# Token mixer written out by batch, with scales kept per batch, entry and shortcut on ScalarE, output products a batch late, and some lag taps as diagonal products on TensorE

## The chip, the cores and the metric

The kernel runs on one core of a Trainium2 chip. The metric is device microseconds of the whole program, lower is better. The median of three runs is 1840.42 us (1838.47 to 1841.76). One more execution was profiled; it took 1830.69 us, and its span from the first to the last instruction is 1828.9 us.

## The reference, cut to what matters

The program is a chain of eight stages on x, of 8 batches, 512 positions and 128 features, in float32. The change touches one stage, the token mixer, which stands between two runs of the same feed-forward. With h as the normalised x:

```python
h  = (x - mean) / sqrt(var + 1e-5)                 # shortcut
xn = h / (rms(h) + 1e-8)
u  = silu(xn @ Wu.T + bu)                          # 256 wide
v  = silu(xn @ Wv.T + bv)                          # 256 wide
o[n]  = sum(coef[lag] * v[n - lag] for lag in 0..n)  # n is the batch; causal
x  = x + (u * o) @ Wo.T + bo + h
```

The mixing runs over the first axis of x, the 8 batches. So batch n needs the v of all batches up to it, and n + 1 taps. The coefficient depends on the feature alone (per partition, with the features laid on partitions). The reference computes this sum by FFT; the kernels compute it by taps.

## The kernel before, in words

x lies in SBUF for the whole program as 32 tiles of 128 positions by 128 features, four tiles a batch. A stage is a block with one program for each engine. Engines meet by semaphores only, and each engine runs its instructions in the order in which its program is written. At the end of a stage all engines meet at a barrier.

The mixer (`token_mixer`, L2343 to L2466) does for each batch: statistics on VectorE (`Norm.stats`, L192 and L196: four and four instructions); on GpSimd a chain of seven small instructions that makes the two factors out of variance and mean (`Norm.powers`, L216 to L223, then `rms_factor`, L2353 to L2357); the normalised x on VectorE (L245) and its scaled copy on ScalarE (L253); four transposes on TensorE (L275) and a copy out of PSUM on ScalarE (L283); four products of 128x512 on TensorE (L2421), each followed by a silu on ScalarE (L2411), two of them u, two of them v; the taps on VectorE, two feature halves of n + 1 taps each, into `mixed` (L2458 for lag 0, L2456 for all others); the product with u (L2462); the output products with the bias on TensorE (L2425, L2429) into one of two PSUM banks by turns; and the sum into x on VectorE (L2446), after GpSimd has added the shortcut (L2399).

The order is written out by `batches`: the front of batch n + 1, then the back of batch n. On VectorE the front is the normalisation of batch n + 1 and the statistics of batch n + 2, and the back is the taps, the product with u, and the sum into x of batch n - 1. On TensorE the front is the transposes and the four products, and the back is the output products of batch n. The v of all batches is kept in `vT`.

The feed-forward stages (`feed_forward`) aren't changed. They are of use here because they hold instructions of the kinds that the changed mixer has: an entry on ScalarE with Identity, a scale and a bias per partition (L2198), and a VectorE instruction with a PSUM input, a scalar per partition and an SBUF input (L2323).

Of the kernel before, what the change touches and what calls it, by code (L numbers as in the profile page):

```python
# [16 lines left out]
F32 = mybir.dt.float32  # L17
# [8 lines left out]
P = 128  # L26
# [2316 lines left out]
def token_mixer(nc, k, name="mix"):  # L2343

    with Stage(nc, name) as st:
        half = st.sb("half", [P, T], F32)
        minus_one = st.sb("minus_one", [P, T], F32)

        def rms_factor(steps, pool, p):
            ms = norm.ms[:, :]
            steps.did(pool.tensor_tensor(ms, ms, half[:, :], ALU.pow))  # L2353
            steps.settle()
            steps.did(pool.tensor_scalar(ms, ms, 1e-8, None, ALU.add))
            steps.settle()
            steps.did(pool.tensor_tensor(norm.factor[:, p, :], ms, minus_one[:, :], ALU.pow))  # L2357

        norm = Norm(st, k.x, 1e-5, "layer_rms", rms_factor, 3)
        bank = [k.ps[:, i, :] for i in range(8)]  # L2360
        feed = Feed(st, k, norm, bank[0])
        ps_uv, ps_out = bank[1:5], bank[5:7]
# [4 lines left out]
        exps = st.counter("exponents")  # L2367
        uv_ready = st.counter("uv_ready", 4, 2)
        silu_ready = st.counter("silu_ready", 4, 1)
        shortcut = st.counter("shortcut_added", 1, 2)  # L2370
        taps = [st.counter(f"taps{c}", 1) for c in range(FEAT)]
        gated_ready = st.counter("gated_ready", FEAT, 2)
        out_ready = st.counter("out_ready", 1, 2)
        x_added = st.counter("x_added", 1, 2)
        norm.also_read = shortcut
        block = st.block()

        def batches(front, back):
            front(0, 0)
            for n in range(B):  # L2380
                if n + 1 < B:
                    front(n + 1, (n + 1) % 2)
                back(n, n % 2)

        @block.sync
        def _(sp):
            st.credit(sp)

        @block.gpsimd
        def _(pool):  # L2390
            norm.setup(pool)
            pool.memset(half[:, :], 0.5)
            pool.memset(minus_one[:, :], -1.0).then_inc(exps.sem, 1)
            hold(pool, exps.sem, 1)

            def back(n, p):
                hold(pool, norm.normed.sem, norm.normed.at(n))
                x = k.x[:, n * T:(n + 1) * T, :]
                pool.tensor_tensor(x, x, norm.out[:, p, :, :], ALU.add).then_inc(shortcut.sem, 1)  # L2399
            batches(lambda n, p: norm.powers(pool, n, p), back)  # L2400

        @block.scalar
        def _(act):
            def front(n, p):
                feed.scalar(act, n, p, uv_ready, uv_ready.at(n - 2))
                for c in range(2 * FEAT):
                    act.wait_ge(uv_ready.sem, uv_ready.at(n, c + 1))
                    if c == 0:
                        act.wait_ge(gated_ready.sem, gated_ready.at(n - 2))
                    to = uT[:, p, c, :] if c < FEAT else vT[:, c - FEAT, n, :]  # L2410
                    act.activation(to, ps_uv[c], ACT.Silu, bias=k.buv[:, c:c + 1]).then_inc(silu_ready.sem, 1)  # L2411
            batches(front, lambda n, p: None)

        @block.tensor
        def _(pe):
            def front(n, p):
                feed.tensor(pe, n, p)
                pe.wait_ge(feed.xT_ready.sem, feed.xT_ready.at(n))
                for c in range(2 * FEAT):
                    pe.wait_ge(silu_ready.sem, silu_ready.at(n - 1, c + 1))  # L2420
                    pe.matmul(ps_uv[c], k.WuvT[:, c * P:(c + 1) * P], feed.xT[:, p, :], start=True, stop=True).then_inc(uv_ready.sem, 1)  # L2421

            def back(n, p):
                pe.wait_ge(x_added.sem, x_added.at(n - 2))
                pe.matmul(ps_out[p], k.onesb, k.bto_rows.unsqueeze(1).to_broadcast([P, T, P]), start=True, stop=True)  # L2425
                for c in range(FEAT):
                    pe.wait_ge(gated_ready.sem, gated_ready.at(n, c + 1))
                    for j in range(T):
                        ins = pe.matmul(ps_out[p][:, j * P:(j + 1) * P], gated[:, p, c, j * P:(j + 1) * P], k.WtoT[:, c * P:(c + 1) * P],  # L2429
                                        start=False, stop=True, skip_group_check=True)  # L2430
                ins.then_inc(out_ready.sem, 1)
            batches(front, back)

        @block.vector
        def _(dve):
            counts = [0] * FEAT

            def did(c, ins):
                ins.then_inc(taps[c].sem, 1)
                counts[c] += 1  # L2440

            def add(n, p):
                dve.wait_ge(out_ready.sem, out_ready.at(n))
                dve.wait_ge(shortcut.sem, shortcut.at(n))
                x = k.x[:, n * T:(n + 1) * T, :].rearrange("p a b -> p (a b)")
                dve.tensor_tensor(x, ps_out[p], x, ALU.add).then_inc(x_added.sem, 1)  # L2446

            def back(n, p):
                dve.wait_ge(silu_ready.sem, silu_ready.at(n))
                dve.wait_ge(gated_ready.sem, gated_ready.at(n - 1))  # L2450
                for lag in range(n + 1):
                    for c in range(FEAT):
# [442 lines left out]
```

## Time and profile before

| | |
|---|---|
| median of 3 runs | 1840.42 us |
| profiled execution | 1830.69 us |
| its span | 1828.9 us |
| busy in the span: TensorE, VectorE, ScalarE, GpSimd | 72%, 59%, 42%, 46% |
| mean granted TensorE clock | 0.854 of full |
| the mixer, from its first VectorE instruction to its last (1618.92 to 1721.46) | 102.54 us |

The busy shares are means over eight stages. The mixer is 6% of the span, between 1618.92 and 1721.46 us. The timeline gives an engine's instructions in order of time, equal ones in a row merged; what stands in square brackets is the time that the engine sat idle before them, with the instruction that ended it. A float32 product on TensorE stands as two records. A granted clock of 1.00 is 2.4 GHz, and 0.50 is 1.2 GHz.

### The profile page before, as it was taken

To read this page: it belongs to the slowest core of one execution; us is meant where nothing else is said; L and a number is where in the kernel's file an instruction comes from. 1 tells how busy PE (TensorE), PEld (TensorE's weight loads), DVE (VectorE), ACT (ScalarE), POOL (GpSimd) and SP (SyncE) were. 2 spreads that over 40 slices of the span, in tenths; PEclk is the share of its full clock that TensorE was granted. 3 is DMA by queue.
4 is the path that set the end of the run, shared out by engine and by line. 5 is a ranking of instruction groups with operands and counts; after the bars stand their busy time and mean duration, and the time that the engine had idled before them with its cause. 6 is when DMAs were issued, how large, how long until landed. Compare 5 with 4: busy or idle time off the path is not lost. (4 is left out here: it accounts for less than half of the span.)

```text
span 1828.9 us, 36163 instructions
## 1 busy us (share of the span) xinstructions
PE 1316.1 (72%) x11164; PEld 849.2 (46%) x11165; DVE 1071.5 (59%) x3170; ACT 774.4 (42%) x1286; POOL 834.1 (46%) x1221
## 2 busy tenths in 40 slices
PE   5763259963988888832299817888899995957486
PEld 3542159961233333322299812333345554734364
DVE  2654425445877877444255456767576634749765
ACT  1221113211466666711033204776655555735274
POOL 2116745533233333357555536766654413447252
PEclk9985579985799999955599956998999998978698
DMA  3004122245323222041122230000000000000001
GB/s 104 0 16 122 42 63 69 67 118 128 71 80 85 66 65 65 3 126 41 58 68 68 59 95 1 1 2 1 2 2 2 1 2 1 1 1 1 1 1 47
DMA packets 87712, 79.80 MB, mean 44 GB/s; under 512 B 11791, under 2 KB 77583, under 8 KB 87280
## 3 DMA queue, kind: packets, MB, share of 16 engines
q1 hardware_dynamic: 76898, 57.16, 12.1%
q0 software_dynamic: 8704, 17.97, 2.9%
q10 hardware_dynamic: 1980, 3.00, 0.8%
q8 instruction: 73, 1.20, 0.3%
q14 instruction: 57, 0.47, 0.1%
HBM read 46.07 MB, written 32.01 MB: 43 GB/s over the span
## 5 line engine op out<-in xcount | busy, mean ns | idle before, releaser
L1146 ACT ACTIVATE grp_pt<-ps 128x1024 f32<-128x1024 f32 (+2 forms) x320 | 244.7, 799 | 212.2 <-PE ps L1223 133.9
L2035 DVE TENSOR_REDUCE soft_mx<-ps 128x2 f32<-128x1024 f32 (+3 forms) x256 | 201.9, 821 | 57.0 <-PE ps L1873 55.7
L680 POOL DMA_INDIRECT products<-moe_product,moe_rows_in x144 | 152.9, 1062 | 151.9 <-DVE moe_product L852 142.3
L1759 ACT ACTIVATE soft_pt<-ps 128x768 f32<-128x768 f32 (+1 forms) x192 | 166.3, 884 | 83.2 <-PE ps L1904 81.6
L707 ACT ACTIVATE moe_hid<-ps 128x512 f32<-128x512 f32 x144 | 85.8, 597 | 249.9 <-PE ps L744 234.2
L1680 POOL TENSOR_SCALAR_AFFINE_SELECT soft_pt<-soft_pt 128x256 f32<-128x256 f32 (+1 forms) x192 | 92.7, 483 | 208.9 <-ACT soft_pt L1759 208.4
L744 PE MATMUL ps<-moe_rT,moe_W_now 128*128 128x128 f32 x1152 | 157.2, 280 | 2.0 <-issue 2.0
L1243 PE MATMUL ps<-grp_pt,grp_vpad 128*32 128x160 f32 (+4 forms) x2048 | 145.6, 393 | 15.9 <-POOL grp_pt L1088 15.7
L753 PE MATMUL ps<-moe_W,moe_hid 128*128 x1152 | 155.2, 278 | 1.3 <-ACT moe_hid L707 1.1
L658 POOL DMA_INDIRECT sorted_rows<-moe_row,moe_target x128 | 124.8, 975 | 50.2 <-issue 35.7
L744 PEld LDWEIGHTS ps<-moe_rT,moe_W_now 128*128 128x128 f32 x1152 | 143.2, 196 | 5.5 <-issue 5.4
L753 PEld LDWEIGHTS ps<-moe_W,moe_hid 128*128 128x128 f32 x1152 | 140.5, 192 | 3.5 <-issue 2.6
L1088 POOL TENSOR_SCALAR_AFFINE_SELECT grp_pt<-grp_pt 128x256 f32<-128x256 f32 (+1 forms) x192 | 102.9, 544 | 70.7 <-ACT grp_pt L1146 69.8
L848 DVE COPY moe_W_now<-moe_W 128x512 f32 x144 | 62.0, 431 | 68.5 <-issue 68.5
L1223 PE MATMUL ps<-grp_qst,grp_kst 32*128 32x160 f16 (+4 forms) x1024 | 96.3, 279 | 7.4 <-ACT grp_pt L1146 5.2
L275 PE MATMUL ps<-pack,moe_normed 128*128 128x128 f32 x64 | 17.8, 433 | 108.2 <-DVE moe_normed L245 108.2
L852 DVE TENSOR_SCALAR moe_product<-ps,moe_rows_in 128x128 f32<-128x128 f32 x144 | 50.6, 351 | 74.2 <-PE ps L753 72.5
L1921 PE MATMUL ps<-soft_pt,soft_vpad 128*32 128x512 f32 (+3 forms) x1024 | 88.8, 442 | 2.1 <-POOL soft_pt L1680 1.9
L1868 PE MATMUL ps<-soft_kst,soft_qst 64*128 64x512 bf16 (+3 forms) x512 | 72.0, 320 | 21.0 <-ACT soft_pt L1759 12.7
L737 PE MATMUL ps<-pack,moe_rows_in 128*128 128x128 f32 x144 | 40.6, 282 | 61.9 <-DMA moe_rows_in<-sorted_rows 61.4
L1243 PEld LDWEIGHTS ps<-grp_pt,grp_vpad 128*32 128x32 f32 x2048 | 51.7, 112 | 61.9 <-POOL grp_pt L1088 24.5
L1223 PEld LDWEIGHTS ps<-grp_qst,grp_kst 32*128 32x128 f16 x1024 | 34.1, 93 | 90.9 <-ACT grp_pt L1146 46.3
(335 smaller groups left out, 2754.2 us busy)
## 6 DMA issues: line engine op xcount, KB each, us to landing
moe_rows_in<-sorted_rows SPq DMA_DIRECT2D x144, 65.0 KB, 1.8
moe_back<-products SPq DMA_DIRECT2D x16, 512.0 KB, 7.2
soft_kst<-soft_scratch_k SPq DMA_DIRECT2D x32, 192.0 KB
moe_W<-in_W SPq DMA_DIRECT2D x2, 2048.0 KB, 8.5
moe_W<-in_W SPq DMA_DIRECT2D x16, 256.0 KB, 6.9
soft_scratch_q<-soft_parts SPq DMA_DIRECT2D x16, 192.0 KB, 2.7
soft_qst<-soft_scratch_q SPq DMA_DIRECT2D x32, 96.0 KB
soft_scratch_k<-soft_parts SPq DMA_DIRECT2D x14, 192.0 KB, 2.8
```

The source lines that it names most:

```text
L658: pool.indirect_dma_start(k.sorted_rows, bass.IndirectOffsetOnAxis(target[:, p, s, j:j + 1], 0), row[:, p, j, s, :], None).then_inc(scatte ...
L680: pool.indirect_dma_start(k.products, bass.IndirectOffsetOnAxis(rows_in[:, u, DEST_COL:DEST_COL + 1].bitcast(U32), 0), product[:, u, :], N ...
L744: ins = pe.matmul(ps_hid[u % 2][:, c * P:(c + 1) * P], W1_now[:, u % 2, c * P:(c + 1) * P], rT[:, u % 2, :], start=True, stop=True)
L753: ins = pe.matmul(ps_out[u % 2][:, 0:P], hid[:, u % 2, c * P:(c + 1) * P], W2[:, bass.ds(e, 1), c * P:(c + 1) * P].rearrange("f a h -> f ( ...
L1088: pool.affine_select(e, e, [[0, 2 if seg < 2 else 4], [1, P]], ALU.is_ge, 0.0, 0, -1).then_inc(kept.sem, 1)
L1146: act.activation(at.pair(pt[:, s % 2, :], pair, seg)[:, :, 0:w], ring[(chunks_before(m) + c) % 2][:, :, 0:w], ACT.Exp, scale=scale).then_i ...
L1223: ins = pe.matmul(ring[now % 2][:, b, col:col + w], kst[32 * g:32 * g + 32, p, j * P:(j + 1) * P], qst[32 * g:32 * g + 32, p, s, j * P:j * ...
L1243: ins = pe.matmul(sums[half][32 * g:32 * g + 32, q:q + w], vpad[:, p, j, par, g, :], at.head(pt[:, s % 2, :], g, seg, a, w), start=(par == ...
L1680: pool.affine_select(e, e, [[0, 2 if seg < 2 else 4], [1, P]], ALU.is_ge, 0.0, 0, -1).then_inc(kept.sem, 1)
L1759: act.activation(LATENT.pair(pt[:, s % 2, :], pair, seg)[:, :, 0:w], ring[second_turn(n, c) % RING3][:, :, 0:w], ACT.Exp, scale=scale).the ...
L1921: ins = pe.matmul(sums[half][32 * g:32 * g + 32, q:q + w], vpad[:, n % 2, par, j, 4 * half + g, :], LATENT.head(pt[:, s % 2, :], g, seg, a ...
L2035: ins = dve.tensor_reduce(mx[:, tile, half, :, r], ring[first_turn(n, d) % RING3][:, :, at:at + keys], AX.X, ALU.max)
```

## The change

The stage gets its own code in place of the shared `Norm` and `Feed`.

- VectorE no longer normalises. It does the statistics two batches ahead, at the start of an iteration, then the taps that are left to it, the product with u, and the sum into x of the batch before.
- GpSimd makes all scales and shifts in a chain of twelve small instructions a batch, kept per batch, and before the second batch six diagonal matrices (the identity times a coefficient). It no longer adds the shortcut.
- ScalarE makes the input of the transposes straight from x (`entries`, with Identity, scale and bias), and turns x into x + h in place (`shortcuts`). The silus of v come ahead of those of u.
- TensorE does the taps of `PE_LAGS` as products of a diagonal matrix with v (11 lags for each of the two feature halves: 22 products of 128x512), a batch ahead; VectorE's first tap adds their sum out of PSUM. The output products of batch n - 1 stand in iteration n, behind the front of batches n + 2 and n + 1 and the taps of n + 1. There is one PSUM bank for them instead of two.

The core of the new code follows; the new `power` also makes `in_scale`, the product of `rstd` and `factor`.

```diff
+    PE_LAGS = [[], [], [1], [1], [1, 2], [1, 2], [1, 2], [1, 2, 3]]
+    DIAGS = 3
+    OUTPUTS = (2, 3, 0, 1)
+    with_taps = [n for n in range(B) if PE_LAGS[n]]
...
+        def taps_through(n):
+            return sum(m + 1 - len(PE_LAGS[m]) for m in range(n))
+        def v_ready(n, c):
+            return silu_ready.at(n, OUTPUTS.index(FEAT + c) + 1)
+        @block.gpsimd
+        def _(pool):
...
+            def power(n):
+                mean, var = mv[:, n, :, 0], mv[:, n, :, 1]
+                pool.wait_ge(stats_done.sem, stats_done.at(n))
+                need(pool, powered, powered.at(n - 1))
+                pool.tensor_scalar(tmp[:, :], var, 1e-5, None, ALU.add).then_inc(powered.sem, 1)
...
+                pool.tensor_tensor(in_shift[:, n, :], tmp[:, :], in_scale[:, n, :], ALU.mult).then_inc(powered.sem, 1)
+                pool.tensor_tensor(x_shift[:, n, :], tmp[:, :], rstd[:, :], ALU.mult).then_inc(powered.sem, 1)
+                pool.tensor_scalar(x_scale[:, n, :], rstd[:, :], 1.0, None, ALU.add).then_inc(powered.sem, 1)
+            power(0)
+            for c in range(FEAT):
+                for lag in range(1, DIAGS + 1):
+                    at = c * B + lag
+                    ins = pool.tensor_scalar(diag[:, c, lag - 1, :], k.ident, k.coef[:, at:at + 1], None, ALU.mult)
+            ins.then_inc(diags_set.sem, 1)
+            for n in range(1, B):
+                power(n)
...
+            def entries(n):
+                p = n % 2
+                act.wait_ge(powered.sem, powered.at(n, 10))
+                need(act, x_turned, x_turned.at(n - 2))
+                for j in range(T):
+                    ins = act.activation(entry[:, p, j, :], k.x[:, n * T + j, :], ACT.Identity, bias=in_shift[:, n, j:j + 1], scale=in_scale[:, n, j:j + 1])
+                ins.then_inc(normed.sem, 1)
+            def shortcuts(n):
+                act.wait_ge(powered.sem, powered.at(n))
+                act.wait_ge(normed.sem, normed.at(n))
+                for j in range(T):
+                    x = k.x[:, n * T + j, :]
+                    ins = act.activation(x, x, ACT.Identity, bias=x_shift[:, n, j:j + 1], scale=x_scale[:, n, j:j + 1])
+                ins.then_inc(shortcut.sem, 1)
+            def copy_xT(n):
+                act.wait_ge(x_turned.sem, x_turned.at(n))
+                need(act, uv_ready, uv_ready.at(n - 2))
+                act.activation(xT[:, n % 2, :], ps_x, ACT.Copy).then_inc(xT_ready.sem, 1)
+            def silus(n):
+                for i, c in enumerate(OUTPUTS):
+                    act.wait_ge(uv_ready.sem, uv_ready.at(n, i + 1))
+                    if c < FEAT:
+                        need(act, gated_ready, gated_ready.at(n - 2, c + 1))
+                    to = uT[:, n % 2, c, :] if c < FEAT else vT[:, c - FEAT, n, :]
+                    act.activation(to, ps_uv[c], ACT.Silu, bias=k.buv[:, c:c + 1]).then_inc(silu_ready.sem, 1)
+            entries(0)
+            copy_xT(0)
+            entries(1)
             for n in range(B):
                 if n + 1 < B:
+                    copy_xT(n + 1)
+                silus(n)
+                shortcuts(n)
+                if n + 2 < B:
+                    entries(n + 2)
...
+            def turn(n):
+                pe.wait_ge(normed.sem, normed.at(n))
+                need(pe, xT_ready, xT_ready.at(n - 1))
+                for j in range(T):
+                    ins = pe.transpose(ps_x[:, j * P:(j + 1) * P], entry[:, n % 2, j, :], k.ident)
+                ins.then_inc(x_turned.sem, 1)
+            def project(n):
+                pe.wait_ge(xT_ready.sem, xT_ready.at(n))
+                for i, c in enumerate(OUTPUTS):
+                    need(pe, silu_ready, silu_ready.at(n - 1, i + 1))
+                    pe.matmul(ps_uv[c], k.WuvT[:, c * P:(c + 1) * P], xT[:, n % 2, :], start=True, stop=True).then_inc(uv_ready.sem, 1)
+            def tap(n):
+                turn_of = with_taps.index(n)
+                pe.wait_ge(diags_set.sem, 1)
+                for c in range(FEAT):
+                    pe.wait_ge(silu_ready.sem, v_ready(n - 1, c))
+                    if turn_of > 0:
+                        pe.wait_ge(taps[c].sem, taps_through(n - 1) + 1)
+                    for i, lag in enumerate(PE_LAGS[n]):
+                        ins = pe.matmul(ps_tap[c], diag[:, c, lag - 1, :], vT[:, c, n - lag, :], start=(i == 0), stop=(i == len(PE_LAGS[n]) - 1))
+                    ins.then_inc(tapped.sem, 1)
+            def output(n):
+                need(pe, x_added, x_added.at(n - 1))
+                pe.matmul(ps_out, k.onesb, k.bto_rows.unsqueeze(1).to_broadcast([P, T, P]), start=True, stop=True)
                 for c in range(FEAT):
                     pe.wait_ge(gated_ready.sem, gated_ready.at(n, c + 1))
                     for j in range(T):
+                        ins = pe.matmul(ps_out[:, j * P:(j + 1) * P], gated[:, n % 2, c, j * P:(j + 1) * P], k.WtoT[:, c * P:(c + 1) * P],
                                         start=False, stop=True, skip_group_check=True)
                 ins.then_inc(out_ready.sem, 1)
...
+            turn(0)
+            turn(1)
+            project(0)
+            for n in range(B):
+                if n + 2 < B:
+                    turn(n + 2)
+                if n + 1 < B:
+                    project(n + 1)
+                if n + 1 in with_taps:
+                    tap(n + 1)
+                if n > 0:
+                    output(n - 1)
+            output(B - 1)
...
+            def stats(n):
+                need(dve, stats_done, stats_done.at(n - 1))
+                for j in range(T):
+                    ins = dve.bn_stats(bn[:, j, :], k.x[:, n * T + j, :])
+                ins.then_inc(stats_done.sem, 1)
+                dve.wait_ge(stats_done.sem, stats_done.at(n, 1))
+                for j in range(T):
+                    ins = dve.bn_aggr(mv[:, n, j, :], bn[:, j, :])
+                ins.then_inc(stats_done.sem, 1)
+            def mix(n):
+                lags = [lag for lag in range(n, -1, -1) if lag not in PE_LAGS[n]]
+                need(dve, gated_ready, gated_ready.at(n - 1))
+                for i, lag in enumerate(lags):
+                    for c in range(FEAT):
+                        at = c * B + lag
+                        v, scale = vT[:, c, n - lag, :], k.coef[:, at:at + 1]
+                        dve.wait_ge(silu_ready.sem, v_ready(n - lag, c))
+                        if i > 0:
+                            dve.wait_ge(taps[c].sem, counts[c])
+                            dve.scalar_tensor_tensor(mixed[:, c, :], v, scale, mixed[:, c, :], ALU.mult, ALU.add).then_inc(taps[c].sem, 1)
+                            counts[c] += 1
+                        elif n in with_taps:
+                            dve.wait_ge(tapped.sem, tapped.at(with_taps.index(n), c + 1))
+                            dve.scalar_tensor_tensor(mixed[:, c, :], v, scale, ps_tap[c], ALU.mult, ALU.add).then_inc(taps[c].sem, 1)
+                            counts[c] += 1
+                        else:
+                            dve.tensor_scalar(mixed[:, c, :], v, scale, None, ALU.mult).then_inc(taps[c].sem, 1)
+                            counts[c] += 1
+            def gate(n):
+                need(dve, out_ready, out_ready.at(n - 2))
+                for c in range(FEAT):
+                    dve.wait_ge(silu_ready.sem, silu_ready.at(n, OUTPUTS.index(c) + 1))
+                    dve.wait_ge(taps[c].sem, counts[c])
+                    dve.tensor_tensor(gated[:, n % 2, c, :], mixed[:, c, :], uT[:, n % 2, c, :], ALU.mult).then_inc(gated_ready.sem, 1)
+            def add(n):
                 dve.wait_ge(out_ready.sem, out_ready.at(n))
                 dve.wait_ge(shortcut.sem, shortcut.at(n))
...
+                x = x_of(n).rearrange("p a b -> p (a b)")
+                dve.tensor_tensor(x, ps_out, x, ALU.add).then_inc(x_added.sem, 1)
+            stats(0)
+            stats(1)
+            for n in range(B):
+                if n + 2 < B:
+                    stats(n + 2)
+                mix(n)
+                gate(n)
+                if n > 0:
+                    add(n - 1)
+            add(B - 1)
```

## Rows read from the trace of the kernel before

**Rows 1.** Stretch: its us; PE, PEld, DVE, ACT, POOL busy (instructions); granted clock; DMA.

```profile
1618.92:1721.46 102.54, 66.25 (x232) 38.78 (x232) 82.87 (x200) 37.91 (x73) 52.99 (x67) 0.75 0.00 1
```

**Rows 2.** Timeline (start, us) of VectorE: the mixer's start and last batches.

```profile
1618.92 0.87 DVE L192 BATCH_NORM_STATS2 mix_bn<-x 128x6 f32<-128x128 f32 x4 [1.60 <-PEq L112]
1619.83 0.38 DVE L196 BATCH_NORM_AGGREGATE mix_mv<-mix_bn 128x2 f32<-128x6 f32 x4
...
1683.90 7.71 DVE L2456 SCALAR_TENSOR_TENSOR mix_mixed<-mix_vT,pack,mix_mixed 128x512 f32<-128x512 f32 x10
...
1705.55 0.68 DVE L2446 TENSOR_TENSOR x<-ps,x 128x512 f32<-128x512 f32 x1
1706.15 0.87 DVE L2458 TENSOR_SCALAR mix_mixed<-mix_vT,pack 128x512 f32<-128x512 f32 x2
1706.94 9.36 DVE L2456 SCALAR_TENSOR_TENSOR mix_mixed<-mix_vT,pack,mix_mixed 128x512 f32<-128x512 f32 x14
1716.21 1.28 DVE L2462 TENSOR_TENSOR mix_gated<-mix_mixed,mix_uT 128x512 f32<-128x512 f32 x2
1717.42 0.68 DVE L2446 TENSOR_TENSOR x<-ps,x 128x512 f32<-128x512 f32 x1
1720.77 0.69 DVE L2446 TENSOR_TENSOR x<-ps,x 128x512 f32<-128x512 f32 x1 [2.67 <-PE ps L2429]
```

**Rows 3.** Timeline of ScalarE in the mixer and the next entry.

```profile
1628.45 0.60 ACT L283 ACTIVATE mix_xT<-ps 128x512 f32<-128x512 f32 x1 [1.21 <-PE ps L275]
...
1700.03 0.69 ACT L2411 ACTIVATE mix_vT<-ps,pack 128x512 f32<-128x512 f32 x1 [0.17 <-PE ps L2421]
...
1726.50 1.65 ACT L2198 ACTIVATE ffn_entry<-x,ffn_xshift,ffn_xrstd 128x128 f32<-128x128 f32 x4 [24.93 <-POOL ffn_xshift L2175]
```

**Rows 4.** Timeline of GpSimd: small instructions of batches 0, 5 and 7.

```profile
1620.36 0.23 POOL L216 TENSOR_SCALAR mix_power_in<-mix_mv 128x4 f32<-128x4 f32 x1 [1.19 <-issue]
...
1623.75 1.04 POOL L2357 TENSOR_TENSOR mix_factor<-mix_ms,mix_minus_one 128x4 f32<-128x4 f32 x1
...
1666.70 1.66 POOL L2355 TENSOR_SCALAR mix_ms<-mix_ms 128x4 f32<-128x4 f32 x1
...
1683.30 0.37 POOL L216 TENSOR_SCALAR mix_power_in<-mix_mv 128x4 f32<-128x4 f32 x1 [2.14 <-DVE mix_mv L196]
...
1688.12 1.39 POOL L2357 TENSOR_TENSOR mix_factor<-mix_ms,mix_minus_one 128x4 f32<-128x4 f32 x1
```

**Rows 5.** Timeline of TensorE in the mixer.

```profile
1629.10 6.29 PE L2421 MATMUL ps<-mix_xT,pack 128*128 128x512 f32 x8 [0.69 <-ACT mix_xT L283]
...
1648.63 3.70 PE L2421 MATMUL ps<-mix_xT,pack 128*128 128x512 f32 x8 [0.69 <-ACT mix_xT L283]
1652.17 0.38 PE L2425 MATMUL ps<-bias_rows,onesb 128*128 128x512 bf16 x1
...
1654.27 0.66 PE L275 MATMUL ps<-pack,mix_normed 128*128 128x128 f32 x4
...
1672.93 1.12 PE L275 MATMUL ps<-pack,mix_normed 128*128 128x128 f32 x4 [3.15 <-ACT mix_normed L253]
1674.73 5.66 PE L2421 MATMUL ps<-mix_xT,pack 128*128 128x512 f32 x8 [0.69 <-ACT mix_xT L283]
...
1716.95 3.78 PE L2429 MATMUL ps<-pack,mix_gated 128*128 128x128 f32 x16 [8.49 <-DVE mix_gated L2462]
```

**Rows 6.** Stretches after one idle time of TensorE.

```profile
1672.00:1674.00 2.00, 1.07 (x4) 0.72 (x4) 1.97 (x9) 0.88 (x4) 1.07 (x2) 0.50 0.00 0
...
1678.00:1680.00 2.00, 2.00 (x5) 0.82 (x4) 2.00 (x5) 1.11 (x2) 2.00 (x2) 0.82 0.00 0
```

**Rows 7.** Groups of GpSimd by shape: busy us, mean ns.

```profile
L1078 POOL COPY grp_vpad<-grp_qkv 128x128 f32<-128x128 f32 x32 | 9.4, 324 | 1.7 <-PE ps L1243 1.7
```

**Rows 8.** Groups of VectorE by shape.

```profile
L2323 DVE SCALAR_TENSOR_TENSOR ffn_h<-ps,pack,ffn_h 128x512 f32<-128x512 f32 x48 | 35.2, 733 | 25.2 <-PE ps L2269 25.2
```

**Rows 9.** Groups of ScalarE by shape.

```profile
L2216 ACT ACT_TABLE_LOAD x2 | 2.6, 1283 | 0.0
```

More of the change, by code:

```diff
@@ L2343, in token_mixer, with need @@
 def token_mixer(nc, k, name="mix"):
-    with Stage(nc, name) as st:
[L2348 to L2359, printed above, removed]
-        bank = [k.ps[:, i, :] for i in range(8)]
-        feed = Feed(st, k, norm, bank[0])
-        ps_uv, ps_out = bank[1:5], bank[5:7]
+    PE_LAGS = [[], [], [1], [1], [1, 2], [1, 2], [1, 2], [1, 2, 3]]
+    DIAGS = 3
+    OUTPUTS = (2, 3, 0, 1)
+    with_taps = [n for n in range(B) if PE_LAGS[n]]
+    def need(eng, signal, value):
+        if value > 0:
+            eng.wait_ge(signal.sem, value)
+    with Stage(nc, name) as st:
+        bank = [k.ps[:, i, :] for i in range(8)]
+        ps_x, ps_uv, ps_out, ps_tap = bank[0], bank[1:5], bank[5], bank[6:8]
+        bn = st.sb("bn", [P, T, 6], F32)
+        mv = st.sb("mv", [P, B, T, 2], F32)
+        tmp = st.sb("tmp", [P, T], F32)
+        rstd = st.sb("rstd", [P, T], F32)
+        factor = st.sb("factor", [P, T], F32)
+        half = st.sb("half", [P, 3, T], F32)
+        in_scale = st.sb("in_scale", [P, B, T], F32)
+        in_shift = st.sb("in_shift", [P, B, T], F32)
+        x_scale = st.sb("x_scale", [P, B, T], F32)
+        x_shift = st.sb("x_shift", [P, B, T], F32)
+        entry = st.sb("entry", [P, 2, T, P], F32)
+        xT = st.sb("xT", [P, 2, S], F32)
+        diag = st.sb("diag", [P, FEAT, DIAGS, P], F32)
         vT = st.sb("vT", [P, FEAT, B, S], F32)
@@ L2366, in token_mixer @@
         gated = st.sb("gated", [P, 2, FEAT, S], F32)
[L2367 to L2375, printed above, removed]
@@ L2376, in token_mixer @@
-        block = st.block()
-        def batches(front, back):
-            front(0, 0)
+        exps = st.counter("exponents", 3)
+        diags_set = st.counter("diags_set")
+        stats_done = st.counter("stats_done", 2)
+        powered = st.counter("power_steps", 12)
+        normed = st.counter("normed")
+        shortcut = st.counter("shortcut")
+        x_turned = st.counter("x_turned")
+        xT_ready = st.counter("xT_ready")
+        uv_ready = st.counter("uv_ready", 4)
+        silu_ready = st.counter("silu_ready", 4)
@@ L2402, in _ @@
[L2402 to L2412, printed above, removed]
+                    copy_xT(n + 1)
@@ L2466, in _ @@
-            norm.stats(dve, 0, 0)
-            batches(lambda n, p: feed.vector(dve, n, p), back)
-            add(B - 1, (B - 1) % 2)
+                x = x_of(n).rearrange("p a b -> p (a b)")
[9 more added lines that the diff above has]
+                    add(n - 1)
```

79 lines of the change are left out of this document (29 added, 50 removed).

## The prediction

> **What bounds the kernel now.** I read the views in this order. The page first: no engine is busy for more than 72% of the span, and the mixer is a small part of it, so only the mixer's own stretch counts. Then that stretch by itself [rows 1]: 102.54 us, in which VectorE is busy for 82.87, TensorE for 66.25, GpSimd for 52.99 and ScalarE for 37.91, at a mean granted clock of 0.75. VectorE paces it: in the timeline its late batches stand end to end, with the taps of the last batch at 1706.94 right behind the sum at 1705.55 and the product with u right behind them [rows 2]. The reader is to see what VectorE does not wait for: the scales of the next batches are made on GpSimd while VectorE is at the taps of this one. Last, the timelines of GpSimd, ScalarE and TensorE, for the durations and hand-overs below.
>
> **The sums over engines, and why I don't go by them.** One tap costs VectorE 0.66 us (14 taps from 1706.94 to 1716.21), one product with u 0.60 (two from 1716.21 to 1717.42), one sum 0.60 (1705.55 to 1706.15), lag 0 as a plain product 0.40 (1706.15 to 1706.94, two), statistics of a batch 1.29 (1618.92 to 1619.83 + 0.38) [rows 2]. After the change VectorE has 4 plain products, 46 taps (72 - 22 - 4), 16 products with u, 8 sums and 8 statistics: 1.6 + 30.4 + 9.7 + 4.8 + 10.3 = 56.8 us. That is 26 us less than 82.87. Twelve of the taps read PSUM; a form of that kind (scalar, one PSUM, one SBUF input) took 733 ns [rows 8] and a tap in SBUF stands for about 740 before overlap, so I cost the source at nothing; by that row 0.1 us a tap either way at most.
> TensorE at 2.4 GHz: transposes 0.66, four products of 128x512 3.54 (1648.63 to 1652.17), output with bias 2.10 (1652.17 to 1654.27) [rows 5], so 6.30 a batch and 50.4 in all, as before; and 22 tap products at 3.54 / 4 = 0.885, 19.5 us more. Neither sum fills 102 us. What decides is the order in which the programs are written.
>
> **The loop that the new order closes.** In iteration n TensorE issues: transposes of n + 2, four products of n + 1, taps of n + 1, output of n - 1. VectorE issues: statistics of n + 2, taps of n, product with u, and the sum of n - 1, which waits for that output. So the statistics of n + 3, first in VectorE's next iteration, stand behind the sum of n - 1, which stands behind the last product of TensorE's iteration n. And TensorE's next iteration starts with the transposes of n + 3, which need ScalarE's entry, which needs ten of GpSimd's twelve steps, which need these statistics. TensorE waits in order, so its four products and its taps, though ready, wait as well. Each of the transposes of batches 4, 5, 6 and 7 (iterations 2 to 5) pays the whole chain once, with TensorE idle. Before, this chain lay beside VectorE's taps.
>
> Price of one such stall: from the last output product to the sum 0.04 (1716.95 + 3.78 to 1720.77 [rows 2, 5]), sum 0.60, statistics 1.29, hand-over 0.15 (1620.21 to 1620.36 [rows 2, 4]), GpSimd p, ScalarE's entry of four 1.65 (the same form in the feed-forward [rows 3]), two hand-overs of about 0.05: 3.8 + p. For p: seven steps undisturbed take 4.43 (1620.36 to 1623.75 + 1.04); the three more are two small products at about 0.28 and a scaling at 0.31, each with its gap (a scaling is 0.23 [rows 4]; both are estimates from rows): 5.3. Beside VectorE's taps seven steps took 6.21 (1683.30 to 1688.12 + 1.39 [rows 2, 4]), 1.40 times as long. VectorE works beside the chain for 3.9 us in iteration 2 (4 taps at 0.66, products with u 1.21), 5.2 in 3 and 4 (6 taps), 6.5 in 5 (8 taps), then it waits. At 1.40 in that time and 1 after it, p is 6.4, 6.8, 6.8, 7.2. Bounds: 5.3, and 8.7 if a scaling is held as at 1666.70 (1.66 us [rows 4]). The four stalls: 10.2 + 10.6 + 10.6 + 11.0 = 42.4 us.
>
> The Trainium skill (GPSIMD Engine Reference, Specifications) says that GpSimd shares its SBUF interfaces with VectorE and contends with VectorE instructions that have two SBUF inputs. The 6.21 against 4.43 agrees. By the rule the first taps of a batch, which take one input from PSUM, would leave GpSimd alone and p would be some 0.4 us shorter; no row here shows it, and the sum goes without it.
>
> **The clock.** TensorE is idle for 10 us and more in each stall. In this trace 3.15 us of idle ahead of the transposes at 1672.93 was enough: granted clock 0.50 (1.2 GHz) from then, and 0.82 in the stretch from 1678 [rows 5, 6]; transposes and products took 1.12 + 5.66 = 6.8 us, and a fully slow pass 1.12 + 6.29 = 7.4, against 0.66 + 3.54 = 4.2 at 2.4 GHz [rows 5]. I take 7.0 for each such pair after a stall, and full speed for what follows it; ends 4.2 and 7.4, and up to twice the price for taps and output if the clock stays down.
> The Trainium skill (TensorE: Matmul & The Clock Gate, What's actually happening) says that the throttled state is the default and activity releases it. That speaks against this change, and the trace agrees with the 0.50 behind the idle time.
>
> **The sum, from the first statistics (0) on.**
> Start: GpSimd begins at 1.44, ten steps to 6.7, twelve to 7.2. The six diagonal matrices come next, ahead of the steps of batch 1: a 128x128 instruction of GpSimd is 324 ns as a copy [rows 7]; I take 0.4 with its gap, 2.4 in all (ends 1.2 and 7). Steps of batch 1 to 14.9, entry to 16.6, and only then the transposes of batch 1, which stand ahead of the first four products. Those end at 16.7 + 7.0 = 23.7. Before, they began at 10.2 (1629.10).
> Iterations 0 and 1: ScalarE has the last silu (0.04 + 0.59), the shortcut (1.55), the entry (1.65), hand-over 0.05: 3.9 between TensorE's products and the next transposes, the silu from [rows 3], the shortcut as an entry. Twice 3.9 + 7.0 makes 45.5. Taps of batch 2 (2 products) 1.77 and output 2.10: 49.4.
> Iterations 2 to 5: stall + 7.0 + taps (1.77, then 3.54 three times) + 2.10: 21.1 + 23.2 + 23.2 + 23.6 = 91.1, so 140.5. ScalarE's last silu and the shortcut (2.2) lie beside taps and output (3.9 or more), and its copy of the transposes (0.60 [rows 3]) beside the products, all at no cost; without that cover the stall hides them.
> Iteration 6: no transposes: 3.54 + 5.31 (6 tap products) + 2.10 = 10.9, so 151.4.
> End: VectorE's sum of batch 5 (0.04 + 0.60) is ahead of the last ten taps (6.62) and two products with u (1.21), then the sum of batch 6 (0.69). The last output waits for that sum, since there is one bank, and runs at 1.2 GHz: 4.2, with the last sum 0.73. Together 14.1: 165.5 us.
> That is 63 us more than 102.54. The profiled execution would be 1830.69 + 63 = 1894 us (its span 1892). It lies 10 us under the median of the runs shown, and the forecast is for runs like those: 1840.42 + 63 = 1903 us.
> VectorE's saved 26 us and the shortcut taken off GpSimd count for nothing here; VectorE waits for TensorE in every iteration.
>
> **Rivals.**
> A, the stalls are hidden after all (the statistics don't wait for the sum as I read it). Then iterations 2 to 5 take TensorE's own 8.1 and three times 9.85, and the stage ends at 112 us: +10, 1850 us. For it: GpSimd needs 7 us a batch, less than TensorE's 10. Against it: the written order. 8%.
> B, the other side: VectorE still sets the pace and its work decides. Its 56.8 us and the 19.7 that it is idle now make 76.5: -26, 1814 us. It decides if the late start (first products at 17.8 in place of 10.2) and the stalls aren't there. For it: VectorE is dense in late batches [rows 2]. 5%.
> C, changes between Silu and Identity reload ScalarE's table. A load is 1.28 us, and the feed-forward, which mixes Identity with Gelu, has only two in 1829 us [rows 9], one a stage. Two loads a batch on the way to the entry: some 15 of them, +19, 1922 us. 4%.
> D, the clock stays at 1.2 GHz for taps and output too: 14 tap products and 4 outputs of iterations 2 to 5 twice as dear, +21, 1924 us. Against it: 0.82 already in the stretch from 1678, five microseconds after such a start [rows 6]. 5%.
> My forecast: 78%.
>
> **Range.** Pairs at full clock seven times would take off 20 us, p at its ends takes off 6 or adds 6, the diagonals take off 1 or add 5. Together, not all at once: 1884 to 1921. A time within 0.2% (3.7 us) of before is what a measurement of this kernel can't tell from none. Slower by more: forecast, C, D and most of A, 93%; same 2%; faster 5%.
>
> **What would show it.** Right: four idle times of TensorE of 10 to 11 us, each ended by ScalarE's entry, with statistics and GpSimd's steps just ahead; VectorE idle ahead of its sums, ended by output products; VectorE busy for about 57 us in some 165; first products near 17.8; clock 0.50 behind each stall. Wrong: statistics of batch 4 that start before the output of batch 0 ends, or transposes that don't wait for the entry. A time under 1870 us would mean that the loop isn't the cause of what happens.

## The result, and the profile after

| | before | after |
|---|---|---|
| median | 1839.45 us (4 runs, 1833.18 to 1841.76) | 1890.24 us (4 runs, 1885.08 to 1900.43) |
| ratio | 1 | 1.0289, 95% interval 1.0238 to 1.0339 |
| profiled execution, its span | 1830.69, 1828.9 us | 1889.10, 1887.3 us |
| the mixer, first to last VectorE instruction | 102.54 us | 160.69 us (1620.66 to 1781.35) |
| TensorE's idle ahead of the transposes of batches 4 to 7 | at most 3.15 us | 10.94, 10.90, 10.90, 11.91 us |

The change makes the kernel 2.9% slower. The forecast was 1903 us, in a range of 1884 to 1921. The profiled executions differ by 58.4 us and the mixers by 58.15, so nearly the whole difference of these two is in the mixer. One of the thirteen executions of the kernel before that stood beside the first four experiments took 4129 us and is left out of the median given there.

First the mixer as one stretch, answering to [rows 1], and the first stall as another (same columns):

```profile
1620.66:1781.35 160.69, 83.95 (x276) 47.59 (x276) 57.21 (x138) 53.26 (x105) 52.15 (x105) 0.74 0.00 0
1667.44:1678.38 10.94, 0.00 (x1) 0.00 (x0) 5.67 (x15) 1.65 (x4) 6.80 (x12) 0.68 0.00 0
```

VectorE is busy for 57.21 us in place of 82.87, and TensorE for 83.95 in place of 66.25. The longest busy time of an engine now fills half of the stretch. In the stall, 10.94 us, TensorE has no busy time. VectorE's statistics, GpSimd's chain and ScalarE's entry stand one behind the other in it; VectorE's taps and products with u lie beside the chain.

VectorE's timeline, answering to [rows 2]: iteration 2 of the loop in full, then most of the sums that waited:

```profile
1667.48 0.69 DVE L2581 TENSOR_TENSOR x<-ps,x 128x512 f32<-128x512 f32 x1 [10.26 <-PE ps L2518]
1668.09 0.86 DVE L2543 BATCH_NORM_STATS2 mix_bn<-x 128x6 f32<-128x128 f32 x4
1668.98 0.38 DVE L2547 BATCH_NORM_AGGREGATE mix_mv<-mix_bn 128x2 f32<-128x6 f32 x4
1669.28 1.38 DVE L2564 SCALAR_TENSOR_TENSOR mix_mixed<-mix_vT,pack,ps 128x512 f32<-128x512 f32 x2
1670.57 1.41 DVE L2560 SCALAR_TENSOR_TENSOR mix_mixed<-mix_vT,pack,mix_mixed 128x512 f32<-128x512 f32 x2
1671.89 1.29 DVE L2575 TENSOR_TENSOR mix_gated<-mix_mixed,mix_uT 128x512 f32<-128x512 f32 x2
1687.81 0.69 DVE L2581 TENSOR_TENSOR x<-ps,x 128x512 f32<-128x512 f32 x1 [14.63 <-PE ps L2518]
...
1732.90 0.69 DVE L2581 TENSOR_TENSOR x<-ps,x 128x512 f32<-128x512 f32 x1 [15.97 <-PE ps L2518]
...
1756.85 0.69 DVE L2581 TENSOR_TENSOR x<-ps,x 128x512 f32<-128x512 f32 x1 [15.60 <-PE ps L2518]
...
1767.44 0.69 DVE L2581 TENSOR_TENSOR x<-ps,x 128x512 f32<-128x512 f32 x1 [2.08 <-PE ps L2518]
...
1780.66 0.69 DVE L2581 TENSOR_TENSOR x<-ps,x 128x512 f32<-128x512 f32 x1 [4.12 <-PE ps L2518]
```

The square brackets are what counts. Before, only the very last sum waited (2.67 us). Now sums wait up to 15.97 us for an output product, and the statistics stand right behind them. The taps that the change spares VectorE would have fitted into these idle times.

GpSimd's timeline, answering to [rows 4]: the diagonal matrices, then the chain of batch 4 (its first, second, third, fourth and tenth step) and one step of batch 7:

```profile
1627.73 3.53 POOL L2439 TENSOR_SCALAR mix_diag<-pack 128x128 f32<-128x128 f32 x6
...
1669.45 0.22 POOL L2413 TENSOR_SCALAR mix_tmp<-mix_mv 128x4 f32<-128x4 f32 x1 [15.25 <-DVE mix_mv L2547]
1669.75 1.04 POOL L2415 TENSOR_TENSOR mix_rstd<-mix_tmp,mix_half 128x4 f32<-128x4 f32 x1
1670.87 0.51 POOL L2417 TENSOR_TENSOR mix_tmp<-mix_mv,mix_rstd 128x4 f32<-128x4 f32 x1
1671.45 1.79 POOL L2419 TENSOR_TENSOR mix_tmp<-mix_tmp,mix_rstd 128x4 f32<-128x4 f32 x1
...
1676.45 0.20 POOL L2431 TENSOR_TENSOR mix_in_shift<-mix_tmp,mix_in_scale 128x4 f32<-128x4 f32 x1
...
1739.56 2.59 POOL L2425 TENSOR_TENSOR mix_factor<-mix_tmp,mix_half 128x4 f32<-128x4 f32 x1
```

ScalarE's timeline, answering to [rows 3] and [rows 9]: the only table load in the mixer, and the entry that ends the first stall:

```profile
1640.17 1.28 ACT L2473 ACT_TABLE_LOAD   x1
...
1676.68 1.65 ACT L2451 ACTIVATE mix_entry<-x,mix_in_shift,mix_in_scale 128x128 f32<-128x128 f32 x4 [10.70 <-POOL mix_in_shift L2431]
```

TensorE's timeline, answering to [rows 5]: from the first four products to the stalls:

```profile
1639.32 5.97 PE L2499 MATMUL ps<-mix_xT,pack 128*128 128x512 f32 x8
1649.14 1.12 PE L2492 MATMUL ps<-pack,mix_entry 128*128 128x128 f32 x4 [3.85 <-ACT mix_entry L2451]
...
1659.62 0.67 PE L2492 MATMUL ps<-pack,mix_entry 128*128 128x128 f32 x4 [3.85 <-ACT mix_entry L2451]
1660.13 3.60 PE L2499 MATMUL ps<-mix_xT,pack 128*128 128x512 f32 x8
1663.56 1.88 PE L2509 MATMUL ps<-mix_vT,mix_diag 128*128 128x512 f32 x4
...
1665.49 1.95 PE L2518 MATMUL ps<-pack,mix_gated 128*128 128x128 f32 x16
1678.38 1.12 PE L2492 MATMUL ps<-pack,mix_entry 128*128 128x128 f32 x4 [10.94 <-ACT mix_entry L2451]
1679.29 4.76 PE L2499 MATMUL ps<-mix_xT,pack 128*128 128x512 f32 x8
...
1698.67 1.12 PE L2492 MATMUL ps<-pack,mix_entry 128*128 128x128 f32 x4 [10.90 <-ACT mix_entry L2451]
...
1720.77 1.12 PE L2492 MATMUL ps<-pack,mix_entry 128*128 128x128 f32 x4 [10.90 <-ACT mix_entry L2451]
...
1744.78 1.12 PE L2492 MATMUL ps<-pack,mix_entry 128*128 128x128 f32 x4 [11.91 <-ACT mix_entry L2451]
```

And the waits of the mixer, summed (who waited for whom: us in total, times, longest):

```profile
DVE x L2581 <- PE ps L2518: 77.7, 7, 16.0
...
PE ps L2492 <- ACT mix_entry L2451: 71.3, 8, 11.9
ACT mix_entry L2451 <- POOL mix_in_shift L2431: 67.3, 6, 14.4
POOL mix_tmp L2413 <- DVE mix_mv L2547: 64.4, 6, 15.5
```

Read together they go round: VectorE's sum waits for TensorE, TensorE for ScalarE's entry, ScalarE for GpSimd's scales, and GpSimd for VectorE's statistics, which stand behind the sum.

### The profile page after: what moved, and what is told of

It reads as the page before. It is cut to its first block and busy times, and to the rows that moved or that the text cites. A ratio compares the mean times of both kernels' runs of the same rounds, so it can differ in the third digit from the quotient of the medians.

```text
span 1887.3 us, 36297 instructions
## 1 busy us (share of the span) xinstructions
PE 1333.8 (71%) x11208; PEld 857.5 (45%) x11209; DVE 1044.6 (55%) x3108; ACT 789.7 (42%) x1318; POOL 833.8 (44%) x1259
## 5 line engine op out<-in xcount | busy, mean ns | idle before, releaser
L1243 PEld LDWEIGHTS ps<-grp_pt,grp_vpad 128*32 128x32 f32 x2048 | 51.7, 112 | 61.3 <-POOL grp_pt L1088 24.1
```

Source lines behind the costliest of these rows:

```text
L1243: ins = pe.matmul(sums[half][32 * g:32 * g + 32, q:q + w], vpad[:, p, j, par, g, :], at.head(pt[:, s % 2, :], g, seg, a, w), start=(par == ...
```

## Experiments

Each mixer is measured like the ones above, from its first statistics to its last sum. It is the better measure here: in the eleven profiled executions the mixer began between 1616.09 and 1629.58 us, by what the unchanged stages ahead of it took, and 105.7 to 107.4 us lay behind it. Where no number of runs is given, the time is that of one execution. The kernel before took 1835.54 us (median of 12) beside the first four experiments, 1833.32 (11) beside the next three and 1833.08 (1) beside the last two.

| run | mixer, us | time, us |
|---|---|---|
| before | 102.5 | 1839.45 (4 runs) |
| after | 160.7 | 1890.24 (4 runs) |
| statistics all ahead | 108.5 | 1838.90 (10 runs) |
| statistics before the sum | 125.3 | 1858.30 |
| no tap products | 152.8 | 1884.76 |
| unread products in the stalls | 153.1 | 1885.54 |
| statistics ahead, early start | 104.8 | 1842.10 |
| statistics ahead, no tap products | 103.7 | 1839.37 |
| reordered | 91.5 | 1819.40 (6 runs) |
| before, with the statistics last | 125.7 | 1851.80 |
| reordered, with the loop put back | 139.2 | 1862.93 |

Theory 1 is the loop of the prediction. Its rivals: the tap products, the late start and the slow clock make the loss (2), or VectorE's work sets the time (3).

### Statistics of all batches ahead

```diff
-            stats(0)
-            stats(1)
+            for n in range(B):
+                stats(n)
             for n in range(B):
-                if n + 2 < B:
-                    stats(n + 2)
                 mix(n)
```

> The changed kernel with VectorE's statistics of all eight batches first, ahead of its loop; nothing else differs. Theory 1 (the loop: the statistics stand behind the sum, and the next transposes behind the statistics): the four idle times of TensorE of 10.9 to 11.9 us go, ScalarE's entry comes within 0.3 us of TensorE's readiness, and the following transposes and products run at 2.4 GHz (4.0 us in place of 5.5 to 6.5). Iterations 2 to 6 become 8.2, 9.9, 9.9, 9.9, 10.7 us, and the mixer ends at 109 to 110 us (160.7 now): 51 us less, about 1838. Theory 2 (tap products, late start and the slow clock make the loss): the mixer stays within 5 us of 160.7.

Measured: mixer 108.5 us; 1838.90 us over ten runs against 1835.54 for the kernel before beside them, ratio 1.0018 with an interval of 0.9989 to 1.0046. TensorE's timeline at the transposes of batches 4 to 7:

```profile
1664.81 0.66 PE L2492 MATMUL ps<-pack,mix_entry 128*128 128x128 f32 x4
...
1672.76 0.66 PE L2492 MATMUL ps<-pack,mix_entry 128*128 128x128 f32 x4
...
1682.12 0.60 PE L2492 MATMUL ps<-pack,mix_entry 128*128 128x128 f32 x4
...
1691.43 0.60 PE L2492 MATMUL ps<-pack,mix_entry 128*128 128x128 f32 x4
```

No row has an idle time ahead of it. Tap products, late start, diagonals and all other edits are still there, and 52.2 of the mixer's 58.2 us are gone; in the time of the whole kernel no loss can be measured. Theory 2 falls as the cause. It keeps at most the 6.0 us by which this mixer is still longer than the one before; its first four products begin at 18.7 us (10.2 before).

### Statistics before the sum

```diff
             stats(1)
+            stats(2)
             for n in range(B):
-                if n + 2 < B:
-                    stats(n + 2)
                 mix(n)
                 gate(n)
+                if n + 3 < B:
+                    stats(n + 3)
                 if n > 0:
                     add(n - 1)
```

> The changed kernel with one step moved on VectorE: the statistics three batches ahead stand in front of the sum of the batch before, no longer behind it. Theory 1: the chain from one output to the transposes now has two iterations of TensorE beside it, so about every second stall goes: stalls of some 5 us at the transposes of batches 5 and 7, none at 4 and 6, mixer about 121 us (160.7 now). Theory 2 (it isn't the place of the statistics): within 5 us of 160.7.

Measured: mixer 125.3 us. TensorE at the transposes of batches 4 to 7:

```profile
1673.16 0.66 PE L2492 MATMUL ps<-pack,mix_entry 128*128 128x128 f32 x4
...
1686.80 1.11 PE L2492 MATMUL ps<-pack,mix_entry 128*128 128x128 f32 x4 [5.82 <-ACT mix_entry L2451]
...
1698.59 0.60 PE L2492 MATMUL ps<-pack,mix_entry 128*128 128x128 f32 x4
...
1713.88 1.12 PE L2492 MATMUL ps<-pack,mix_entry 128*128 128x128 f32 x4 [5.82 <-ACT mix_entry L2451]
```

Every second stall is gone and the others are 5.82 us, as the loop has it. A place in the order ahead of one wait is worth 35 us. The mixer is 4 us longer than expected: the two stalls together are 1.6 us longer, and the transposes and products of batch 3 (1662.68 to 1669.15) took 6.5 us at the slow clock, 3.9 in the changed kernel.

### No tap products

```diff
-    PE_LAGS = [[], [], [1], [1], [1, 2], [1, 2], [1, 2], [1, 2, 3]]
+    PE_LAGS = [[], [], [], [], [], [], [], []]
```

The six diagonal matrices are not made either.

> The changed kernel with all taps back on VectorE (no diagonal matrices, no tap products). Theory 1: in the loop the tap products stand on TensorE's way from the transposes to the output, while VectorE waits in any case; taking them away shortens the way by 1.8 + 3 x 3.5 + 1.8 us in iterations 1 to 5 and the start by 3.5, and gives some back at the end, where VectorE has 22 more taps to do: the mixer at 148 us in place of 160.7. Theory 3 (VectorE's work sets the time, so the moved taps help): VectorE gets 22 x 0.66 less 0.3 for each of 12 = some 11 us more, mixer at 170 or more.

Measured: mixer 152.8 us, 8 less than after. The sign is theory 1's; 5 us of the size are missing. The stalls grew, since GpSimd's chain now has more of VectorE's taps beside it (11.46, 11.70, 11.59, 12.62 us in place of 10.94 to 11.91; 2.7 us in all), and the transposes and products behind them took 26.2 us in place of 24.1. Theory 3 falls: 22 more taps on VectorE, and the mixer is shorter.

### Unread products in the stalls

```diff
                 if n + 2 < B:
+                    if n >= 2:
+                        need(pe, xT_ready, xT_ready.at(n + 1))
+                        for j in range(11):
+                            pe.matmul(ps_x, k.ident, vT[:, 0, 0, :], start=True, stop=True)
                     turn(n + 2)
```

> The changed kernel with 11 products of 128x512 that nobody reads, put on TensorE ahead of the transposes of batches 4, 5, 6 and 7, into the bank that the transposes then overwrite (11 x 0.885 = 9.7 us, under the 10.9 of a stall). If the clock that falls in a stall has a price, the transposes and products that follow take 4.0 us in place of 5.5, 5.6, 6.5 and 6.4: 8 us less, mixer at 153 us, at stalls of the same length. If it has none, 160.7 stays; if the products don't fit in the stall, it gets longer.

Measured: mixer 153.1 us. TensorE around the first stall, the unread products first:

```profile
1672.68 9.61 PE L2530 MATMUL ps<-mix_vT,pack 128*128 128x512 f32 x22
1683.79 0.67 PE L2492 MATMUL ps<-pack,mix_entry 128*128 128x128 f32 x4 [1.50 <-ACT mix_entry L2451]
1684.29 3.60 PE L2499 MATMUL ps<-mix_xT,pack 128*128 128x512 f32 x8
1687.73 1.88 PE L2509 MATMUL ps<-mix_vT,mix_diag 128*128 128x512 f32 x4
```

Behind them the transposes and the four products took 0.50 + 3.44 us (1683.79 to 1687.73) in place of 0.91 + 4.60 (1678.38 to 1683.89 in the profile after). The four pairs of transposes and products behind the stalls took 15.7 us in place of 24.1: 8.3 us (from unrounded times) of the loss are the fallen clock, a consequence of the stalls and no cause beside them. The mixer is only 7.6 us shorter, mostly because the three pairs ahead of the first stall came out 1.0 us longer here. They did so too with the statistics ahead; so the 7.6 and the 44.6 of the stalls together are the 52.2 that the first experiment gave back (160.7 to 108.5).

### Statistics ahead, early start

```diff
-            power(0)
+            for n in range(4):
+                power(n)
             for c in range(FEAT):
...
-            for n in range(1, B):
+            for n in range(4, B):
                 power(n)
...
             turn(0)
-            turn(1)
             project(0)
+            turn(1)
```

> Statistics of all batches first; the diagonal matrices made after the scales of batch 3 in place of batch 0; the first four products ahead of the transposes of batch 1. It measures the start by itself. First products at 10.4 us of the mixer in place of 18.6; the silus of batch 0 still stand behind the copy of batch 1's transposes on ScalarE (from 18), so only half of it comes through: transposes of batch 2 at 23.7 in place of 27.8, mixer at 104.5 us against 108.5. If the start were hidden by something later, 108.5 stays.

Measured: mixer 104.8 us. The first products came at 10.3 us, the transposes of batch 2 at 24.4 (27.9 with statistics ahead alone). As expected, less than half of the start comes through: 3.5 of 8.4 us.

### Statistics ahead, no tap products

This has the edits of the first and the third experiment together.

> Statistics of all batches first, as in the run with that alone, and all taps on VectorE, so no tap products and no diagonal matrices. It asks what the tap products are worth once the loop is open. If TensorE's way still sets the time (theory 1): iterations 1 to 4 are 1.8 to 3.5 us shorter, the start 3.5 shorter, the last three batches are VectorE's and longer: mixer at 104 us against 108.5 with the tap products. If VectorE's work sets it once the loop is open (theory 3): 22 taps more, 11 us, so 119.

Measured: mixer 103.7 us, 4.8 less than with the tap products. Of these, 3.4 are the start without the diagonal matrices (first products at 15.2 us, 18.7 with them). The tap products themselves bring nothing in this order: they are 1.4 us the worse. The starts of the transposes tell why. Without tap products the middle iterations take 7.95 us each (1671.91 to 1679.87), in which TensorE waits 1.85 us for the entry, which stands behind the silus and the shortcut on ScalarE. With statistics ahead an iteration with one lag takes the same 7.95 (1664.81 to 1672.76), and one with two lags 9.3 (1682.12 to 1691.43): the first lag lies in TensorE's wait, the second does not. From batch 6 on VectorE works without a gap up to the wait for the last output. Batch 6 in its timeline, one lag as a plain product and six as taps, two halves each:

```profile
1703.77 0.87 DVE L2562 TENSOR_SCALAR mix_mixed<-mix_vT,pack 128x512 f32<-128x512 f32 x2
1704.56 8.03 DVE L2555 SCALAR_TENSOR_TENSOR mix_mixed<-mix_vT,pack,mix_mixed 128x512 f32<-128x512 f32 x12
```

### Reordered

```diff
-    PE_LAGS = [[], [], [1], [1], [1, 2], [1, 2], [1, 2], [1, 2, 3]]
+    PE_LAGS = [[], [], [1], [1], [1], [1], [1, 2], [1, 2, 3]]
...
                 silus(n)
-                shortcuts(n)
                 if n + 2 < B:
                     entries(n + 2)
+                shortcuts(n)
...
-                if n + 1 in with_taps:
-                    tap(n + 1)
                 if n > 0:
                     output(n - 1)
+                if n + 1 in with_taps:
+                    tap(n + 1)
...
                 mix(n)
+                if n == B - 1:
+                    add(n - 1)
                 gate(n)
-                if n > 0:
+                if 0 < n < B - 1:
                     add(n - 1)
```

With statistics ahead and the early start; the silus of batch 0 ahead of the copy for batch 1, and in the last batch the sum from PSUM as an instruction of its own behind the others.

> The changed kernel put in an order that follows from theory 1: all statistics first; the diagonal matrices after the scales of batch 3; the first four products ahead of the transposes of batch 1; on ScalarE the entry ahead of the shortcut; on TensorE the output of n - 1 ahead of the taps of n + 1; 9 lags in place of 11 on TensorE; in the last batch VectorE starts with the taps from SBUF, adds TensorE's sum last, and the sum of batch 6 comes ahead of the product with u. Theory 1 (TensorE's own way of about 66 us at 2.4 GHz, a start of 10 and an end of some 7, with no chain in between): mixer at 88 to 92 us, 12 us under the kernel before (102.5), about 1824. Rival (GpSimd's chain of 5.8 us a batch and ScalarE's order hold the early batches back, and the clock stays down): 98 to 103, no gain that can be measured.

Measured: mixer 91.5 us; 1819.40 us against 1833.32 for the kernel before beside it, ratio 0.9920 (0.9906 to 0.9933). It is 0.8% faster than the kernel before, with an interval clear of 1, and so faster than the changed one. The mixer as one stretch (columns as above):

```profile
1621.06:1712.54 91.48, 71.61 (x268) 41.58 (x268) 61.66 (x144) 52.19 (x105) 51.60 (x105) 0.86 0.00 1
```

TensorE is now busy for 71.61 of 91.48 us at a granted clock of 0.86 (0.74 after the change, 0.75 before). So a kernel with diagonal products, the entry on ScalarE and scales per batch can be faster than the one before, if nothing closes a loop. Which of them pays was not taken apart.

### The kernel before, with the statistics last

```diff
                 if n >= 1:
                     add(n - 1, 1 - p)
+                if n + 2 < B:
+                    norm.stats(dve, n + 2, p)
```

The statistics of n + 2 in the front are taken out for it.

> The kernel before with one step moved: VectorE's statistics of batch n + 2 stand at the end of its iteration, behind the sum of n - 1, in place of ahead of the taps of n (and the ninth, unused statistics are gone, 1.3 us). Output products are not late here, so the sum doesn't wait. Theory 1 (what counts is what lies beside GpSimd's chain): now nothing does, so VectorE waits 0.15 + 4.4 us for the scales at each of the normalisations of batches 2 to 7, 27 us in all where it waits 3 now: mixer at 125 us (102.5 now). Rival (only the late output makes a stall, the place of the statistics alone doesn't): 101 to 103.

Measured: mixer 125.7 us. One of the six waits, in VectorE's timeline:

```profile
1676.81 0.86 DVE L192 BATCH_NORM_STATS2 mix_bn<-x 128x6 f32<-128x128 f32 x4
1677.70 0.38 DVE L196 BATCH_NORM_AGGREGATE mix_mv<-mix_bn 128x2 f32<-128x6 f32 x4
1682.63 2.05 DVE L245 TENSOR_SCALAR mix_normed<-x,mix_mv,mix_rstd 128x128 f32<-128x128 f32 x4 [4.55 <-POOL mix_factor L2357]
```

All six are 4.54 or 4.55 us. So late outputs are not needed for a loss: it is enough that nothing lies beside GpSimd's chain. Late outputs make it the larger one.

### Reordered, with the loop put back

```diff
-            for n in range(B):
-                stats(n)
+            stats(0)
+            stats(1)
             for n in range(B):
+                if n + 2 < B:
+                    stats(n + 2)
                 mix(n)
```

> The reordered kernel, with one thing put back: the statistics two batches ahead at the start of VectorE's iteration, behind the sum, as in the changed kernel. Theory 1: the loop is there again at batches 4 to 7, but the output now stands ahead of the taps of the next batch, so these lie beside it: stalls of 10.9 less 1.8, 1.8, 1.8 and 3.5 us, 35 in all, and 1.5 to 2.5 us more for each following pair at the fallen clock: mixer at 132 to 135 us (91.5 with statistics ahead). Rival (the other edits of that kernel took the stalls away): under 100.

Measured: mixer 139.2 us, 47.7 more for the place of six statistics. The expectation was 4 to 7 us short, 4.0 of it in the stalls. Of these, 1.7 are my own slip: ahead of the transposes of batches 4 to 7 stand the taps of 2 to 5, one lag each, so 1.8 us comes off each stall and never 3.5. Another 1.2 are GpSimd's ten steps for batches 6 and 7, 8.2 and 8.4 us in place of 7.15 and 8.2 after the change; with 9 lags on TensorE two more of VectorE's taps lie beside each of them. TensorE at these transposes:

```profile
1663.77 1.11 PE L2495 MATMUL ps<-pack,mix_entry 128*128 128x128 f32 x4 [9.24 <-ACT mix_entry L2452]
...
1683.34 1.12 PE L2495 MATMUL ps<-pack,mix_entry 128*128 128x128 f32 x4 [9.18 <-ACT mix_entry L2452]
...
1702.68 1.12 PE L2495 MATMUL ps<-pack,mix_entry 128*128 128x128 f32 x4 [10.19 <-ACT mix_entry L2452]
...
1722.80 1.12 PE L2495 MATMUL ps<-pack,mix_entry 128*128 128x128 f32 x4 [10.40 <-ACT mix_entry L2452]
```

The stalls are 39.0 us in all; of the remaining 8.7, the four pairs behind them make 8.2 (23.6 us, 15.5 in the reordered kernel), which is the slow clock.

## Why the prediction was right, step by step

| term of the sum, us | forecast | measured |
|---|---|---|
| to the transposes of batch 1 | 16.7 | 17.75 |
| ScalarE between iterations, twice | 7.8 | 7.7 |
| transposes and four products, seven times | 49.0 | 41.5 |
| the four stalls | 42.4 | 44.6 |
| taps and outputs, iterations 1 to 5 | 24.7 | 24.4 |
| iteration 6 | 10.9 | 10.75 |
| end | 14.1 | 13.95 |
| mixer | 165.5 | 160.7 |

The terms are divided at the starts of TensorE's groups in its timeline. The mechanism was right: the first experiment changes only the place of the statistics and 52 of the 58 us go; the last puts only that back and 47.7 us return.

**Transposes and products after an idle time** were mis-sized, 7.5 us too dear. I took 7.0 for all seven. They took 6.9, 6.6, 3.9, 5.5, 5.6, 6.5 and 6.4. One didn't run slow at all (1659.62, 0.67 and 3.60), though ScalarE had kept TensorE idle for the same 3.85 us as at 1649.14, where the transposes took 1.12. The granted clock was 1.00 in this pair, and 0.71, 0.69, 0.60 and 0.60 in the four behind the stalls, where I had close to 0.50 throughout.

**The stalls** were 2.2 us longer than forecast. From its first step to the end of the tenth GpSimd took 7.2, 7.15, 7.15 and 8.2 us where I had 6.4, 6.8, 6.8 and 7.2. The dearest excess of each chain is in one step, the one beside VectorE's products with u: 1.79 us for a small product that takes 0.20 undisturbed, 1.00 twice for a scaling that takes 0.23, and 2.59 for a power that takes 1.04. Together these are 4.7 of the 8.5 us that the four chains took over 5.3 each. My factor of 1.40 was from a chain with no such step beside products with u; the bound with a held scaling [rows 4] has the right mechanism, since that scaling ended (1668.36) as VectorE's products with u did (1668.26). In size its 8.7 us was the nearer number for the last chain alone.

The Trainium skill (GPSIMD Engine Reference, Specifications) names VectorE instructions with two SBUF inputs among those that contend. The trace now agrees in both directions: beside the taps that read PSUM (1669.28 to 1670.66) the first two steps took 0.22 and 1.04, undisturbed values, and beside the taps from SBUF right behind them the third took 0.51 where 0.20 is undisturbed. The first step of [rows 4] with 0.37 us is no such case: beside it stood the plain product of lag 0 (1683.13 to 1683.90), not a tap, which the prediction's 6.21 us "beside VectorE's taps" passes over.

**The start**: the six diagonal matrices took 3.53 us, 0.59 each, where I took 0.4 from a copy. It lies inside the bound.

**The clock**: it fell behind every stall as forecast, and rose sooner. Its price there is 8.3 us, where the forecast had 11.2 (four times 7.0 less 4.2). The Trainium skill (TensorE: Matmul & The Clock Gate, What's actually happening) has activity release the throttle; the unread products agree, since with TensorE busy at a granted clock of 1.00 up to 1.50 us before them, the transposes and products behind ran at 1.00 too (1683.79 to 1687.73).

**Rivals**: A and B are out by the stalls. C is out: ScalarE loaded its table once (1640.17) though Identity and Silu alternate for eight batches. D is out: in iterations 2 to 5 taps and outputs ran at 2.4 GHz (1.88 for two tap products).

**The absolute time** was 13 us too high, the difference of the medians 12 us too large (63 against 51). Of the mixer's own size 5 us are missing. The rest is the place of the profiled executions among the runs: the one of before was 9 us under the median of before, which I took for an offset that both kernels would share, and the one of after lies 1 us under its own median. So the profiled pair differs by 58.4 us and the medians by 51.

Left open: how much of the reordered kernel's gain each of its edits brings was not taken apart, nor how much the kernel before would gain from statistics ahead alone. Why the same 3.85 us of idle was followed by either clock is open too.

## What to carry to other kernels

A sum over engines says what a stage could take; the written order says what it takes. When work is put a batch late or a batch ahead, follow for each engine what stands behind the waiting instruction, and go on from engine to engine until the walk ends or comes round to where it started. Small steps that feed the next front (statistics, powers) belong ahead of any wait for a late result, above all when an idle time at the start has room for all of them.

## What the runs showed of the hardware

- A GpSimd instruction on 128x4 elements was held until VectorE's products of two SBUF tensors beside it were over: 1.79 us for 0.20 (1671.45 to 1673.24, the products until 1673.18), 1.00 for 0.23. A power took 2.59 for 1.04. Beside taps from SBUF a small product took 0.51 to 0.58.
- An idle time of 3.85 us on TensorE was followed by transposes at 1.2 GHz in one iteration and at 2.4 GHz in the next; with statistics ahead the two came in the other order (0.66 at 1644.70, 1.12 at 1654.34). The granted clock during the transposes was 0.50 or 1.00.
- A VectorE tap with its second tensor in PSUM took as long as one from SBUF (1.38 and 1.41 us for two).
